# The high half of the probabilities: copied from the first exponential's result instead of computed by a second exponential of the score bank

## The reference

```python
x = x + attn(layernorm(x))   # qkv = h @ Wqkv + b; softmax(q k^T / sqrt(32)) v; @ Wo + bo
x = x + ffn(layernorm(x))    # (silu(h @ Wg^T) * (h @ Wu^T)) @ Wd^T
```

## Time and profile before

| | |
|---|---|
| median of 3 runs | 3000.97 us (2999.91 to 3004.09) |
| the profiled execution | 3001.82 us, span 3000.0 us |
| TensorE matmul (PE) busy | 2954.2 us, 98% of the span |
| VectorE (DVE) | 2180.4 us, 73% |
| ScalarE (ACT) | 1660.0 us, 55% |
| GpSimd (POOL) | 1393.7 us, 46% |
| granted TensorE clock | 0.998 |

### The profile page before, as it was taken

The page is one execution under the profiler, slowest core; times in us unless marked ns, Lnnn a source line. Parts: engine busy times, 40 slices in busy tenths (PEclk is TensorE's granted clock), DMA queues, the critical chain, the costliest instruction groups (busy, mean ns, idle before and its releaser), DMA issues.

```text
span 3000.0 us, 39212 instructions
## 1 busy us (share of the span) xinstructions
PE 2954.2 (98%) x13728; PEld 2335.6 (78%) x13728; DVE 2180.4 (73%) x3175; ACT 1660.0 (55%) x3039; POOL 1393.7 (46%) x998
## 2 busy tenths in 40 slices
PE   7999999999999999999999999999999999999999
PEld 7777777777777777777677878888888888888887
DVE  6788888888788888888885488866665666555653
ACT  2588877778788888888874143333333323332221
POOL 1346555554555555556552244444354444535730
PEclk9999999999999999999999999999999999999999
DMA  5545445454454554645845735522532223857874
GB/s 205 173 135 163 142 139 184 131 170 128 128 174 131 156 169 140 192 130 150 253 134 178 240 109 193 189 102 100 233 135 100 100 104 118 262 177 252 268 244 132
DMA packets 328376, 492.10 MB, mean 164 GB/s; under 512 B 34746, under 2 KB 178234, under 8 KB 320116
## 3 DMA queue, kind: packets, MB, share of 16 engines
q1 hardware_dynamic: 328180, 489.60, 51.4%
HBM read 318.58 MB, written 169.87 MB: 163 GB/s over the span
## 4 chain that ended last, share of the span: by engine, by line
PE 89%; DVE 6%; DMA 1%; ACT 1%; issue 1%; POOL 1%; SPq 0%; DVEq 0%; ACTq 0%
PE ps L901 20%; PE ps L902 20%; PE ps L903 20%; PE ps L985 7%; PE ps L997 7%; PE ps L1002 7%; PE ps L969 7%; DVE mx L1342 1%; DVE pl L1364 1%; PE ps L935 1%; DVE wl L1316 1%; ACT ph L1124 0%; ACT pu L1123 0%; SPq L1634 0%; DVE bl L1427 0%
## 5 line engine op out<-in xcount | busy, mean ns | idle before, releaser
L1551 POOL TENSOR_TENSOR pl<-pu,ph 128x512 fp32r<-128x512 f32 x504 | 679.6, 1350 | 677.8 <-ACT ph L1124 677.5
L1342 DVE TENSOR_REDUCE mx<-ps 128x1 f32<-128x512 f32 x1024 | 695.6, 685 | 165.9 <-PE ps L969 159.0
L1123 ACT ACTIVATE pu<-ps 128x512 f32<-128x512 f32 x1024 | 617.6, 603 | 281.8 <-PE ps L985 279.0
L1124 ACT ACTIVATE ph<-ps 128x512 fp32r<-128x512 f32 x1024 | 616.8, 602 | 0.0
L1364 DVE TENSOR_TENSOR pl<-pu,ph 128x512 fp32r<-128x512 f32 x520 | 423.9, 817 | 72.3 <-ACT ph L1124 70.9
L901 PE MATMUL ps<-bh,gh 128*128 128x512 f32 x1208 | 471.3, 390 | 5.3 <-DVE bl L1427 2.5
L903 PE MATMUL ps<-bl,gh 128*128 128x512 f32 x1208 | 470.1, 389 | 0.0
L902 PE MATMUL ps<-bh,gl 128*128 128x512 f32 x1208 | 470.0, 389 | 0.0
L985 PE MATMUL ps<-qst,kst 128*128 128x512 f32 x1024 | 404.5, 395 | 4.3 <-ACT ph L1124 3.5
L997 PE MATMUL ps<-ph,vt 128*65 128x512 f32 x1024 | 407.8, 398 | 0.7 <-ACT uu L1130 0.6
L969 PE MATMUL ps<-kst,qst 128*128 128x512 f32 x1024 | 403.4, 394 | 1.6 <-DVE mx L1342 1.3
(11 more groups left out here) (143 smaller groups left out, 5167.7 us busy)
## 6 DMA issues: line engine op xcount, KB each, us to landing
graw<-in_wgu SPq DMA_DIRECT2D x42, 1024.0 KB, 5.2
sraw<-a_d SPq DMA_DIRECT2D x56, 704.0 KB, 4.9
qst<-q_d SPq DMA_DIRECT2D x192, 128.0 KB
kst<-k_d SPq DMA_DIRECT2D x192, 128.0 KB
a_d<-hs SPq DMA_DIRECT2D x88, 256.0 KB, 2.1
traw<-in_wd SPq DMA_DIRECT2D x77, 256.0 KB, 5.3
tt<-in_wd SPq DMA_DIRECT2D x77, 256.0 KB, 5.3
q_d<-stg SPq DMA_DIRECT2D x64, 256.0 KB, 2.5
```

The source lines that it names most:

```text
L1123: e.activation(pu[sl][:, :], bk[:, :], ACT.Exp, scale=SCALE).then_inc(s["a_p"], 1)
L1124: e.activation(ph[sl][:, :], bk[:, :], ACT.Exp, scale=SCALE).then_inc(s["a_ph"], 1)
L1342: e.reduce_max(mx[:, j % 2, t, half:half + 1], ps[bank_of["a", j, t, half]][:, :], AX.X).then_inc(s["v_mx"], 1)
L1551: e.tensor_tensor(pl[sl][:, :], pu[sl][:, :], ph[sl][:, :], ALU.subtract).then_inc(s["g_pl"], 1)
```

## The change

ScalarE's second instruction of a tile no longer reads the bank and takes no exponential: it copies `pu` from SBUF into `ph`, with the same rounding, after waiting for `pu` (its own instruction just before). L985 then waits for `pu` of tile n − 2, not for `ph`.

```diff
@@ -981,7 +981,7 @@
                     if t == 0:
                         pe.wait_ge(f"d_m{j % 2}", 32 * (j // 2 + 1))
                         pe.wait_ge("v_one", 2)
-                    pe.wait_ge("a_ph", n - 2)
+                    pe.wait_ge("a_p", n - 2)
                     e.matmul(ps[(n - 1) % 2][:, :], kst[j % 3][:, tile_of(t)], qst[j % 3][:, halves(half)],
                              start=True, stop=True).then_inc(s["p_st"], 1)
 
@@ -1121,7 +1121,8 @@
                     act.wait_ge("p_st", n)
                     act.wait_ge("p_pv", n - NPU)
                     e.activation(pu[sl][:, :], bk[:, :], ACT.Exp, scale=SCALE).then_inc(s["a_p"], 1)
-                    e.activation(ph[sl][:, :], bk[:, :], ACT.Exp, scale=SCALE).then_inc(s["a_ph"], 1)
+                    act.wait_ge("a_p", n)
+                    e.activation(ph[sl][:, :], pu[sl][:, :], ACT.Copy).then_inc(s["a_ph"], 1)
```

## The result

The changed kernel takes 3006.5 us (median of 20 runs, 3004.1 to 3007.7) against 3000.8 us (20 runs, 2996.6 to 3005.7): ratio 1.0017, interval 1.0011 to 1.0022, or +3.3 to +6.6 us. It is slower, by less than the forecast of +9. The 0.2% that the prediction took as the least that can be told apart lies inside the interval, and the interval's lower end (3004.1 us) still lies within the prediction's *hidden* case (up to 3005).

A forecast was written before the change was run, and what follows sets the result against it. TensorE was taken to bound the attention stretch, busy 1483.1 of 1500 us. The terms 6.6 + 3 + 1 + 0.5 − 2 gave +9 us, a forecast of 3010 us, range 2999 to 3026.

The forecast's parts named there:

- hidden: Rival: ScalarE's 283 us idle absorb everything, the earlier bank pays for few stalls; 2998 to 3005 us, chance 0.34.
- The pair: ScalarE's two instructions per tile: held 1.15 us, 0.18 more than now, 184 us over 1024 tiles.
- The outline of what hides it: ScalarE's 283 us idle hide the 184 us on average; sign: its wait for L985 down 150 us or more.
- Step 1: Head ends: `uu` 0.55 us later, so L997 waits, +6.6 us; sign: from 8 places to 25 or more.
- Step 2: VectorE gets `ph` 0.16 us later, so TensorE waits longer for `mm` and `mx`: 3 + 1 us.
- Step 3: TensorE's waits at L1002 for `pl` from VectorE: 0.5 us.
- Step 4: L985: bank free 0.49 us earlier for the same `pu` start, but ScalarE further behind; −2 us, bounds 0 and −11.9.
- Step 5: New waits for `ph` on TensorE at L997, already met: zero.
- 3036: Rival: ScalarE becomes the bound in stretches, a `uu` comes 0.9 us late; +35 us, chance 0.09.

The follow-up runs named there:

- e2: Kernel before the change, only the second exponential also waits until the first has ended: 3010.4 us, ratio 1.0033.
- e1: Changed kernel, but L985 waits for `ph` of tile n − 2 again, so the bank is released late: 3011.8 us, ratio 1.0036.
- e12: Changed kernel, copy of tile n − 1 placed behind `pu` of tile n, `pl` one tile later in the list: 3000.2 us, ratio 0.9995.
- e7: Changed kernel, ScalarE's `uu` put between `pu` and `ph` in 100 of 128 places: 3009.1 us, ratio 1.0029.
- e11: Changed kernel, turning of maxima (L976) 4 units late except heads 57 to 59, and `uu` between `pu` and `ph`: 2996.9 us, ratio 0.9987.
- e6: Changed kernel, TensorE's turning of a head's maxima (L976) 4 units late instead of 2: 3006.3 us, ratio 1.0017.
- e10: Changed kernel, turning of maxima (L976) 4 units late instead of 2 except heads 57 to 59: 2996.4 us, ratio 0.9986.
- e4: Kernel before the change, with an added, already met wait for `ph` at each L997: 3000.3 us, ratio 1.0003.
- e3: Kernel before the change, plus a third ScalarE instruction per tile on 8 columns, after `ph`; L985 waits for it: 3012.2 us, ratio 1.0037.
- e5: Kernel before the change, TensorE's turning of a head's maxima (L976) 4 units late instead of 2: 2999.4 us, ratio 0.9993.

## Why the prediction was right, and where it was off

*What bounds, and the direction.* Right: TensorE bound the stretch before and after, and the change lost by making it wait.

*The pair.* Worked out from rows of other instructions: a hand-over of 0.03 to 0.04 us (32 ns measured), a copy of 0.61 to 0.62 us (0.632), 1.15 us per tile (1.14 to 1.16). e2 shows that this is the cause: the wait alone, with nothing else changed, costs 1.0033, as much as e1 (1.0036), which has the copy as well. e12 agrees from the other side, 0.9995 instead of 1.0017, but with `pl` moved as well.

*The outline of what hides it.* Right: ScalarE's wait for L985 fell by 163.7 us (184 predicted as the sum, at least 150 as the sign).

*Step 1, `uu`.* Right in kind. The sign was weight-load waits up from 8 places to 25 or more: there are 23, and 30 with the waits of the matmuls themselves. At the boundary worked the delay was larger (0.74 against 0.55 us), since that working began with an empty queue; over all boundaries it was smaller, a median of 0.36 us. The term was 6.6 us; by the starts of the matmuls TensorE lost 4.5 us more at L997. How much of the whole loss hangs on it is another question: e7 and e11 took half of these waits away and gained nothing.

*Step 2, VectorE.* The sign (longer waits for `mm`) came, 17 us more of idle, where the sum had 3 and its bounds were 5.9, or 11 for a delay of 0.3 us. The working let only the 37 waits there were grow; 32 new ones came. In lost time it is 6.9 us at L976. But as a term that adds up with the others it fails: e6 and e10 remove these waits and the change costs as much as ever. The waits for `mx` at L969, predicted to grow, fell from 6.3 to 4.6 us.

*Step 3, `pl` to L1002.* 0.5 us in the sum; the weight loads' waits for VectorE's `pl` stayed at 0.8 us of idle, in 2 places instead of 3.

*Step 4, the bank.* The net was in the right direction (11.9 to 6.6 us of idle; in lost time −3.7 us, for −2 in the sum). The working saw only the waits there were. e1 shows what it left out: with the longer pair and no early release, 74 waits would have stood there. The release is worth some 6 us of a gross loss of some 11 (e1); the prediction's sum has neither number.

*Step 5.* Right, by e4.

*The sum.* +9 predicted, +3.3 to +6.6 measured. By the starts of the matmuls the sum was too high at `uu` (6.6 for 4.5), at `mx` (+1 for −1.3) and at the bank (−2 for −3.7), had nothing for L901 (−2.3), and was too low at `mm` (3 for 6.9). That it came within 4 us of the measured time is in part luck: errors of opposite sign cancelled. The terms were also added as if TensorE's waits were independent. They are not: e7 and e11 each removed one kind of wait, and others took its place with no gain. A wait ahead of one place would give the engines behind the next place time to catch up; that reading fits, but no run isolates it.

*The range and the chances.* The range's upper end, 3026, is called the first half of the way to 3036; half way from the forecast of 3010 is 3023. And the *hidden* case was near: the time is 1.5 us above its upper end. The measured 0.17% lies within 0.2%, which had a chance of 0.38; slower than that had 0.57.

## What to carry to other kernels

On ScalarE here, a second instruction that waits for the engine's own last result gives up the overlap with it and adds a hand-over; when the two sources cost nearly the same, that wait is the price. Putting the reader one item later took it away (0.99 us a tile), at the price of waits further on. Count what the longer pair would have cost at the resource it releases early, not only the waits that stand there now. When removing many small waits changes nothing, look for one new long one: here a single wait of 12 us for a DMA, with some 2 us at half the clock behind it, hid most of a gain of 10 to 12 us, and an exception for three heads brought it out. And sum lost time by the starts of the engine that bounds, not by idle rows: of 17 us more of idle for `mm`, 6.9 us were lost.

## What the runs showed of the hardware that was not expected

A wait of ScalarE for its own last result had the same price in the three places tried, 32 ns of idle before each: before the copies of the changed kernel, before the exponentials of e2 and, by this row (busy us, mean ns | idle before), before the third instruction of e3, on 8 columns. What is lost beside it is the overlap, 0.10 us.

```profile
L1126 ACT ACTIVATE ps<-ps 128x8 f32<-128x8 f32 x1016 | 164.6, 162 | 32.3
```

On TensorE, 1024 waits that are already met cost nothing that 11 runs can tell (e4, 0.9995 to 1.0012).

TensorE's granted clock fell from 1.00 to 0.50 during single waits of 12 us (e5) and 9 us (e6), and stood at 1.00 again from 1476.5 us (e5) and 1480.7 us (e6), the matmuls having resumed at 1471.87 and 1475.77.
